# Router in halves, weights and tables carried into the stages: the heads of three stages of a five-stage kernel

## What is computed

```
h = layernorm(x) * (1 + ca) + sa;  x = x + ga * attention(h)
h = layernorm(x) * (1 + cb) + sb;  x = x + gb * feed_forward(h)
```

```
# experts 1: 8 routed (inner 128) + 1 shared, on xn = rmsnorm(x) * w_ln2
probs = softmax(xn @ Wgate + expert_bias);  top 2, divided by their sum -> comb
out = shared(xn) + sum_e comb[e] * (silu(xn @ Wg[e]) * (xn @ Wu[e])) @ Wd[e]
# rotary attention, one head of 256, causal
q, k, v = h @ wq.T, h @ wk.T, h @ wv.T
q = q * cos + rotate_half(q) * sin;  k = k * cos + rotate_half(k) * sin
softmax(q @ k.T / 16, causal) @ v
# experts 2: 16 routed (inner 64) + a shared one (inner 512)
scores = sigmoid(h @ router_w.T)
choice: scores + bias; per group of 4 the sum of its 2 best, 2 best groups, in these the 4 best
weights = scores of the 4, divided by their sum
```

## Time and profile before

| | before |
|---|---|
| median of 3 runs | 2570.85 us (2563.58 to 2577.55) |
| the profiled execution's own time | 2572.85 us |
| its span in the trace | 2571.1 us |
| PE busy | 2352.5 us (91%) |
| DVE, ACT, POOL busy | 1802.2, 1378.4, 931.2 us |
| mean granted clock of PE | 0.966 |

### The profile page before, as it was taken

How to read it: one execution, slowest core, us unless ns; L and a number is a source line. 1 busy time by engine, 2 the same in 40 slices (tenths; PEclk the granted TensorE clock), 3 DMA queues, 4 the chain that set the end, 5 groups by cost and what they waited for, 6 DMA issues and landing times. The chain is left out here.

```text
span 2571.1 us, 46412 instructions
## 1 busy us (share of the span) xinstructions
PE 2352.5 (91%) x16756; PEld 1955.7 (76%) x16756; DVE 1802.2 (70%) x3346; ACT 1378.4 (54%) x2607; POOL 931.2 (36%) x1042
## 2 busy tenths in 40 slices
PE   7998877999999999999999889999778888999999
PEld 5777654777788777777777678888667776888887
DVE  6888874897778777877787566666566657666664
ACT  5666543777777777777777643332234443333322
POOL 1233334364547454645444312122256641010000
PEclk9999987999999999999999989999889998999999
DMA  4011104433353344333433162332301113132221
GB/s 144 19 44 53 30 14 138 131 112 101 107 150 109 109 111 145 111 105 108 139 108 108 47 200 57 104 97 72 120 9 36 35 62 109 35 78 49 71 58 42
DMA packets 193188, 223.68 MB, mean 87 GB/s; under 512 B 37160, under 2 KB 156608, under 8 KB 189312
## 3 DMA queue, kind: packets, MB, share of 16 engines
q1 hardware_dynamic: 192960, 220.71, 29.9%
HBM read 150.75 MB, written 55.47 MB: 80 GB/s over the span
## 5 line engine op out<-in xcount | busy, mean ns | idle before, releaser
L1271 DVE TENSOR_REDUCE l_negmax<-l_mx 128x1 f32<-128x512 f32 (+3 forms) x608 | 393.2, 652 | 69.0 <-PE l_mx L1665 66.0
L1284 DVE TENSOR_TENSOR l_Plo<-l_s,l_Phi 128x512 fp32r<-128x512 f32 x576 | 391.4, 680 | 12.6 <-ACT l_s L1520 11.6
L1516 ACT ACTIVATE l_Phi<-l_s 128x512 fp32r<-128x512 f32 x576 | 339.1, 589 | 106.1 <-PE l_s L1689 104.3
L1520 ACT ACTIVATE l_s<-l_s 128x512 f32<-128x512 f32 x576 | 341.3, 592 | 0.0
L1665 PE MATMUL l_mx<-l_KK,l_QA 128*128 128x512 f32 (+3 forms) x768 | 281.5, 406 | 42.8 <-DMA l_QB<-l_qd 30.0
L1700 PE MATMUL l_o<-l_Phi,l_V 128*128 128x256 f32 x1152 | 302.1, 284 | 1.7 <-ACT l_Osb L1528 1.7
L1700 PE MATMUL l_o<-l_Plo,l_V 128*128 128x256 f32 x1152 | 299.7, 282 | 0.0
L2836 ACT ACTIVATE m_hidhi<-m_h 128x512 fp32r<-128x512 f32 x168 | 106.2, 632 | 358.4 <-DVE m_h L2685 358.4
L1687 PE MATMUL l_s<-l_QA,l_KK 128*128 128x512 f32 x576 | 250.8, 435 | 0.7 <-DMA l_QB<-l_mrow 0.4
L1700 PEld LDWEIGHTS l_o<-l_Phi,l_V 128*128 128x128 f32 x1152 | 219.5, 191 | 17.1 <-DVE l_Plo L1284 7.1
L1700 PEld LDWEIGHTS l_o<-l_Plo,l_V 128*128 128x128 f32 x1152 | 218.4, 190 | 15.7
(11 more groups left out here) (473 smaller groups left out, 6352.0 us busy)
## 6 DMA issues: line engine op xcount, KB each, us to landing
l_qd<-l_qs SPq DMA_DIRECT2D x256, 128.0 KB, 2.3
l_QA<-l_qd SPq DMA_DIRECT2D x64, 512.0 KB, 3.6
l_QB<-l_qd SPq DMA_DIRECT2D x64, 256.0 KB, 4.4
l_R<-l_rd SPq DMA_DIRECT2D x128, 128.0 KB, 2.9
m_spread<-m_combs SPq DMA_DIRECT2D x62, 256.0 KB, 5.3
m_spread<-m_combs SPq DMA_DIRECT2D x124, 128.0 KB, 5.0
xs<-next_store SPq DMA_DIRECT2D x32, 256.0 KB, 2.0
l_rps<-l_rp SPq DMA_DIRECT2D x128, 64.0 KB, 1.9
```

The costliest lines, as they stand in the source:

```text
L1271: v.tensor_reduce(negmax[:, n % 2, at + h0:at + h1], piece_of(number, chunk), AX.X, ALU.max, negate=True).then_inc(reduced, 1)
L1284: v.tensor_tensor(Plo[:, s % 3, x].rearrange("p h q -> p (h q)"), S2[s % 2][:, x * HALF:(x + 1) * HALF], Phi[:, s % 3, x].rearrange("p h q ...
L1516: a.activation(Phi[:, u // 2 % 3, u % 2].rearrange("p h q -> p (h q)"), scores_of(u), ACT.Exp, scale=L_D ** -0.5).then_inc(exped, 1)
L1520: a.activation(scores_of(u), scores_of(u), ACT.Exp, scale=L_D ** -0.5).then_inc(exped, 1)
```

## The change

**Carried over.** Five small tables (the token scale, and router weights and bias of both expert stages) are loaded in the latent stage, at its slot 4, into buffers of their own. In the first expert stage's jobs 24 and 36 the rotary stage's wk and then wq are split into `kept` (ScalarE the high part, VectorE one job later the low part); `pair` is loaded anew each time behind that (jobs 30 and 42), with wq and then wv. In the rotary stage's batch 1 the first two loads of the second expert stage's weights are issued into `nxt.staged`. `kept` later serves as the second stage's `spread`.

```diff
+        self.small, self.staging = signal("small"), [signal(f"staging{i}") for i in range(2)]
+        self.token_scale = sb("token_scale", [P, KC])
+        self.router = {"m0": sb("m0_wr", [P, KC, MOE0["experts"]]), "m1": sb("m1_wr", [P, KC, MOE1["experts"]])}
+        self.router_bias = {"m0": sb("m0_rb", [P, MOE0["experts"]]), "m1": sb("m1_rb", [P, MOE1["experts"]])}
+        self.kept = self.staged = None
...
+    def load_small(self, sp, W):
+        sp.dma_start(self.token_scale[:, :], W["m0_ln"]).then_inc(self.small, 16)
+        for name in ("m0", "m1"):
+            sp.dma_start(self.router[name][:, :, :], W[name + "_wr"]).then_inc(self.small, 16)
+            sp.dma_start(self.router_bias[name][:, :], W[name + "_rb"].partition_broadcast(P)).then_inc(self.small, 16)
...
+                    nxt.load_small(sp, W)
...
+                if nxt.stage == 2:
+                    nxt.kept = sb("kept", [P, 4, KC, C], F32R)
+                if nxt.stage == 3:
+                    nxt.staged = sb("staged", [P, 2, 4 * C])
```

```diff
-    AT = (1, 1, 2, 2, 3, 3, 4, 4, 4, 5, 6, 6, 6, 7, 7, 8)
+    AT = (0, 0, 1, 2, 2, 3, 3, 4, 4, 5, 6, 6, 6, 7, 7, 8)
+    AT_SECOND = (1, 1, 2, 2, 3, 3, 4, 4, 4, 5, 6, 6, 6, 7, 7, 8)
...
-                    self.slots[TT * (b - 1) + self.AT[i]].append(t)
+                    self.slots[TT * (b - 1) + (self.AT if b > 1 else self.AT_SECOND)[i]].append(t)
...
-        return self.turns[t][0] == "key" or self.turns[t][1] > 0
+        return self.turns[t][0] == "key" or self.turns[t][1] > 0 or self.turns[t][2] == 1
...
+        wv = nxt.pair
+        wkhi, wklo, wqhi, wqlo = (nxt.kept[:, i] for i in range(4))
+        wvhi, wvlo = (sb(n, [P, KC, C], F32R) for n in ("wvhi", "wvlo"))
...
             for h in range(NH):
                 sp.dma_start(cos[:, :, half(h)], K["rcos"][:, :, half(h)]).then_inc(tload[h], 16)
                 sp.dma_start(sin[:, :, half(h)], K["rsin"][:, :, half(h)]).then_inc(tload[h], 16)
-                if h == 0:
-                    sp.dma_start(wv[:, :, :], W["r_wv"]).then_inc(wload[2], 16)
-            for b in (1, 0, 2):
+                load(1, h)
+            for b in (0, 2):
                 for h in range(NH):
                     load(b, h)
...
                 if b == 1:
+                    for i, n in enumerate(("m1_wg", "m1_wu")):
+                        sp.dma_start(nxt.staged[:, i, :], W[n][:, 0:4].rearrange("p a k m -> p (a k m)"))\
+                            .then_inc(nxt.staging[i], 16)
...
-            split(0)
-            split(1)
-            for t in range(L.HEAD):
+            split()
+            for t in range(2):
+                tokens_low(t)
+            for t in range(2, L.HEAD):
                 project(t)
-                if t == 5:
-                    split(2)
+            measure(1, 0)
...
+                    if j in (4, 5) and b + 2 < B:
+                        measure(b + 2, j - 4)
+                        if j == 5:
                             aggregate(b + 2)
-                    if j in (0, 2) and b + 1 < B:
-                        normalize(b + 1, j // 2)
+                    if g in (0, 2):
+                        normalize(1, g // 2)
+                    if j == 7 and b + 2 < B:
+                        normalize(b + 2, 0)
+                    if j == 1 and 1 <= b < B - 1:
+                        normalize(b + 1, 1)
...
-                elif 0 <= g < TILES and j == 7 and b + 2 < B:
+                elif 0 <= g < TILES and j == 6 and b + 2 < B:
                     inverse_root(b + 2)
...
-            for t in range(L.HEAD):
-                if t == 2:
-                    for n in range(3):
-                        split(n)
-                project(t)
+            split()
+            for t in range(2):
+                tokens_high(t)
+            rotated_high(2)
+            for t in (6, 7):
+                tokens_high(t)
+            for t in (3, 4, 5):
+                rotated_high(t)
...
-                if g == -1:
+                if g == -2:
                     exp(0)
```

```diff
         CHAIN = 12 if first else 28
+        SECOND = NS + (1 if first else 5)
+        KEEP = {24: 0, 36: 1} if first else {}
...
-        first_banks = (Z, Cb, acc[0], acc[1])
+        first_banks = (Gb[1], Ub[1], acc[0], acc[1])
...
-            sp.dma_start(rbias[:, :], W[name + "_rb"].partition_broadcast(P)).then_inc(wload, 16)
+            if first:
+                load_weights(0)
+                load_weights(1)
+            load_weights(2)
             sp.dma_start(lower[:, :, :], K[name + "_lower"]).then_inc(wload, 16)
...
+                if n in RELOAD:
+                    sp.wait_ge(kept_lo, RELOAD[n] + 1)
+                    sp.dma_start(nxt.pair[:, :, :], W[("r_wq", "r_wv")[RELOAD[n]]]).then_inc(nxt.weight, 16)
...
-            chains = {0: routing(0)}
+            chains = {0: routing(0), 1: routing(1)}
+            if first:
+                next(chains[0])
+                next(chains[1])
+                split(3)
+                split(4)
+            else:
+                next(chains[0])
+                split(3)
+                next(chains[0])
+                split(4)
+            LATER = {NS: 4} if first else {NS + 1: 2, NS + 2: 2, NS + 3: 2, NS + 4: 2}
...
+                    for _ in range(4 if first else 1 if n in (0, 3) else 2):
                         next(chains[0])
+                for _ in range(LATER.get(n, 0)):
+                    next(chains[1])
...
+                if n == SECOND:
+                    comb_out(1)
+                if n - 1 in KEEP:
+                    keep_low(KEEP[n - 1])
...
+                split(0)
+            first_tokens(1)
+            if first:
+                split(1)
+                probabilities(0)
+                split(2)
+                probabilities(1)
+                split(3)
+            else:
+                probabilities(0)
+                split(2)
+                probabilities(1)
+                split(3)
+            split(4)
+            split(5)
             for n in range(JOBS + 1):
                 b, r = ahead(n)
                 if b is not None and 5 <= r < 9:
                     tokens(b, r - 5)
-                if n == 0 and first:
-                    probabilities(0)
                 if n >= 1:
...
-            def comb_turn(b):
-                pe.wait_ge(chain, CHAIN * (b + 1))
-                pe.transpose(Z[0:TE, 0:P], comb[:, :, :].rearrange("p t e -> p (t e)"), ident[:, :])\
+            def comb_turn(p):
+                pe.wait_ge(chain, links_after(p))
+                if p == 1:
+                    pe.wait_ge(comb_ready, 1)
...
+                if n == SECOND:
+                    comb_turn(1)
```

318 lines of the change are left out of this document (182 added, 136 removed).

## The result

| | before | changed kernel |
|---|---|---|
| median, first comparison | 2571.27 us (7 runs) | 2559.78 us (7 runs, 2548.95 to 2566.08) |
| ratio, 95% interval | | 0.9944 [0.9929, 0.9959] |
| median, second comparison | 2575.97 us (24 runs) | 2563.36 us (10 runs) |
| ratio, 95% interval | | 0.9963 [0.9948, 0.9978] |
| profiled executions | 2572.85, 2579.40 us | 2548.95, 2556.19 us |

The account below looks back on a forecast made before the run. PE, busy 91% of the span, bounds the kernel; only its waits and lower clock can shrink. Terms 5.7 + 9.5 + 5.2 + 3.6 - 0.5 = 23.5 us took 2572.85 to 2549.4, forecast median 2548 us, range 2536 to 2560.

Parts of the forecast that it names:

- Rotary head, 9.5 us forecast: Rotary stage's head: values' weight split goes first, first score 8.9 us sooner, batch 1 turned 9.5 us sooner; bounds 4 and 11.
- Rival 2: Rotary head: GpSimd's longer rotations slow VectorE, head gains 0.5 instead of 9.5, passages 0; 2562 us; chance 0.10.
- one of the signs that I had named for being wrong: Rotary head: VectorE steps of 0.69 us reading 1.3 and more would show the forecast wrong.
- Rotary passages, 5.2 us: Rotary stage, batches 2 and 3: turning a slot sooner saves 2.6 us a passage, twice 5.2; bounds 0 and 9.
- stays nearly as it is (2.4): Rotary passages: the keys' wait of 2.28 us was to stay nearly unchanged, at 2.4.
- First expert head, 5.7 us with bounds 3 and 8: First expert stage's head: early small loads and half-size ranks let PE turn batch 1 at 1517.5 instead of 1523.23.
- starts the first half's ranks at about 1497.5: First expert head: VectorE, after key steps and two weight splits, begins the first half's ranks at about 1497.5.
- the two later splits that I had costed at nothing: First expert stage's later jobs: two ScalarE copies, two VectorE differences, two loads cost nothing; without PE's cover, two times 0.69 us.
- Second expert head, 3.6 us: Second expert stage's head: shares turned 12 us sooner, shrinking to 3.6 at batch 1's turn; bounds 0 and 9.
- Rival 1: Both expert heads: VectorE becomes the bound, first head gives 3 us and second 0; 2554 us; chance 0.13.
- the 0.86 that I had named: Second expert head: PE's clock below 0.86 in this stretch would show the forecast wrong.
- Latent stage, 0.5 lost: Latent stage: five small loads occupy SP's queue 3 us or less and cost 0.5 us; bounds 0 and 3.

Follow-up runs that it names:

- The experiment on the split: Kernel best1 (the changed kernel plus four edits) with VectorE's split of the values' weights back behind the rotated keys and queries: 2553.14 us (0.9921).
- the kernel with the old slots: Changed kernel with all batches using the old slots (1, 1, 2, 2, ...) for their turns, rows still normalised sooner: 2556.73 us (0.9925).
- the three executions at 37.3 to 37.4 us: Three later executions with the changed kernel's code in the first expert head; batch 1 turned 37.3 to 37.4 us after the stage's start.
- The run with late loads: Changed kernel with the five small loads issued as the first expert stage's first work instead of in the latent stage: 2566.47 us (0.9971).

## Why the prediction came out as it did

- **Rotary head, 9.5 us forecast: right, and for the stated reason.** 10.3 us in the first pair of profiles, 9.7 in the second; the first score 9.3 us sooner where I had 8.9. The matmul of the mask ahead of the first score waits 0.57 us for the queries' low part, the order that I had, and that part ends 21.6 us after the start (22.1 forecast). The experiment on the split shows the mechanism. Rival 2 did not decide it, though VectorE's stretched steps are still there (1.63 and 1.79 us at L2004 and L2011), one of the signs that I had named for being wrong: giving the queries back to VectorE cost 3.1 us in the head.
- **Rotary passages, 5.2 us: wrong.** At most 0.9 us a passage (0.6 in the first profile), and over seven executions nothing clear of their spread. The step that failed is the keys' wait: "stays nearly as it is (2.4)", and it was 3.27. The second query's wait did shrink as I had it (1.75 to 0.28, forecast about 0.3), but I had no term for the waits that came in its place, 1.14 us at the first query and 0.90 at the turning. PE stood still 9.4 us a batch, where the kernel with the old slots has 6.0. I had followed the shifted slots as one thing with the earlier rows and never priced the earlier rows alone, which give 4 to 5.5 us a batch.
- **First expert head, 5.7 us with bounds 3 and 8: too large, below its lower bound.** 2.3 us in the first pair of profiles, 0.7 in the second; with the three executions at 37.3 to 37.4 us it is about 1 us by the means (37.0 against 37.9), within the spread of 1.6 us that the kernel before shows. The half chain took 3.08 us where I had 3.1 (ten steps with 0.16 us fixed in each would give 3.0). What failed is the step before it, "starts the first half's ranks at about 1497.5", 13.0 us after the stage's start: they began 16.8 after it. The two weight splits were 4.4 us for 1.9, and waited 1.33 for ScalarE; that is the whole delay of 3.8. It does not settle the head, though: batch 1 is turned 3.4 to 4.4 us later than forecast, and the ranks put ahead of the splits give back only 0.9 to 1.9 of that. What holds the rest is open. I had put GpSimd's contention into the rotary head alone, where the row that showed it stood; here the same thing happened, and rival 2's mechanism was real at another place than I gave it. The Trainium skill (GPSIMD Engine Reference, section Key points) has VectorE contend with GpSimd where its instruction has two SBUF inputs; with 0.96 against 1.84 us and 0.95 against 2.60 the runs agree.
- **First expert stage, the jobs: missing.** No term had the 0.03 us by which every job got longer, 2.1 us in 71 jobs, and the two later splits that I had costed at nothing make PE wait 0.6 us once.
- **Second expert head, 3.6 us: right.** 3.3 us in the first pair of profiles, 4.3 in the second, and by the account given, twelve us sooner at the first turn (ten measured) and bound by VectorE's second chain. PE turned the second half's shares 63.0 us after the start, where I had that half ready at 62.6. Rival 1 was half true for this head: PE waited 3.45 us there (2.19 in the second profile), over the 2 us that I had named as a sign of being wrong, but the head still gained. The clock, 0.85, also lies just under the 0.86 that I had named. In its steady part a job fell from 4.22 to 4.19 us, another 2.5 us in the stage that I had not foreseen. The distance between weights and tokens changed here too, from 114,400 to 97,792 bytes; that this is the cause was not tried in this stage.
- **Latent stage, 0.5 lost:** cannot be told within its spread. The run with late loads gives no sign of more than 3 us. On SP's queue the five loads stand for 2.5 us, within the 3 that I had put without working it out.
- **Sum.** Faster was right, the size too large: both comparisons lie at the 0.5% that I called what a measurement can tell, one at each side. The three stages gave 15.6 us of 24.0; the medians say 11.5 and 12.6. Where the 3 to 4 us between these lie stays open, since the part before the first expert stage spreads by 20 us. The misses were both in terms where I had followed one engine's order closely and let another's durations stand as they had been.
